# Moving an output copy, a transposed drive and the next batch's norm pieces within the state loop of a fused kernel

## What is computed

```python
def step(h, inp):
    dt_t, B_t, C_t, x_t = inp
    dA = jnp.exp(dt_t[:, :, None] * A)
    h = dA * h + (dt_t * x_t)[:, :, None] * B_t[:, None, :]
    y = jnp.einsum('bds,bs->bd', h, C_t)
    return (h, y)
...
y = y + xc * D_param
y = y * silu(z)
return jnp.einsum('bld,od->blo', y, out_proj_w)
```

## Time and profile before

| | |
|---|---|
| median of 3 runs | 1814.51 us (1811.84 to 1815.16) |
| the profiled execution | 1811.03 us, its span 1809.2 us |
| TensorE matmul, busy | 1623.4 us (90%) |
| TensorE weight load | 1052.8 us (58%) |
| VectorE | 1138.1 us (63%) |
| ScalarE | 1033.0 us (57%) |
| GpSimd | 1051.4 us (58%) |

### The profile page before, as it was taken

How to read it: one execution, slowest core, us unless ns; L and a number is a source line. 1 busy time by engine, 2 the same in 40 slices (tenths; PEclk the granted TensorE clock), 3 DMA queues, 4 the chain that set the end, 5 groups by cost and what they waited for, 6 DMA issues and landing times. The chain is left out here.

```text
span 1809.2 us, 23458 instructions
## 1 busy us (share of the span) xinstructions
PE 1623.4 (90%) x6777; PEld 1052.8 (58%) x6822; DVE 1138.1 (63%) x1344; ACT 1033.0 (57%) x2054; POOL 1051.4 (58%) x562
## 2 busy tenths in 40 slices
PE   5589998979999888999897999878999999999997
PEld 2244445644445553444563444556688888888896
DVE  2799988489898579898758999846422222222222
ACT  5868875878974888986687887431122222222222
POOL 0599890278995158999037899400355555555543
PEclk9799999999999999999998999987799999999999
DMA  3355650156652056664015575552022222222222
GB/s 105 113 184 211 222 184 1 52 190 210 233 188 94 0 162 208 208 211 175 2 65 203 197 241 192 214 222 73 25 37 39 36 40 35 35 38 38 38 31 26
DMA packets 76670, 216.14 MB, mean 119 GB/s; under 512 B 12397, under 2 KB 31158, under 8 KB 73239
## 3 DMA queue, kind: packets, MB, share of 16 engines
q1 hardware_dynamic: 60662, 196.25, 31.4%
q0 software_dynamic: 15904, 18.66, 6.5%
HBM read 193.47 MB, written 19.82 MB: 118 GB/s over the span
## 5 line engine op out<-in xcount | busy, mean ns | idle before, releaser
L477 PE MATMUL psum<-HC_sb,ident_sb 128*128 128x512 f32 x768 | 365.9, 604 | 16.4 <-DVE HC_sb L1618 8.9
L2033 ACT ACTIVATE hgt_sb<-psum_moe,b_sb 128x256 f32<-128x256 f32 (+1 forms) x312 | 116.5, 456 | 424.4 <-PE psum_moe L1933 424.4
L477 PE MATMUL psum<-experts_sb 64*128 64x512 f32 (+6 forms) x838 | 277.4, 566 | 60.7 <-DVE HC_sb L1618 20.7
L1198 ACT ACTIVATE experts_sb<-experts_sb 128x128 f32<-128x128 f32 x800 | 255.8, 388 | 36.0 <-PE psum L480 34.3
L1933 PE MATMUL psum_moe<-XGT_sb,w1s_sb 128*128 128x256 f32 (+1 forms) x1248 | 254.3, 362 | 1.3 <-DVE XGT_sb L2170 0.9
L2185 DVE TENSOR_TENSOR YS_sb<-psum_moe,b_sb 128x256 f32<-128x256 f32 x71 | 30.2, 425 | 357.3 <-PE psum_moe L1933 357.3
L1933 PE MATMUL psum_moe<-experts_sb,hgt_sb 128*128 x1136 | 251.7, 379 | 0.7 <-DVE YS_sb L2185 0.7
L1608 DVE TENSOR_TENSOR_SCAN experts_sb<-experts_sb,psum 128x1024 f32<-128x1024 f32 x100 | 227.1, 2271 | 39.7 <-PE psum L480 26.0
L1908 POOL DMA_INDIRECT out<-YS_sb,scat_sb x71 | 128.6, 1811 | 202.3 <-DVE YS_sb L2189 187.6
L1933 PEld LDWEIGHTS psum_moe<-XGT_sb,w1s_sb 128*128 128x128 f32 x1248 | 218.9, 191 | 27.1 <-DVE w1s_sb L2176 1.2
L477 PEld LDWEIGHTS psum<-HC_sb,ident_sb 128*128 128x128 f32 x768 | 141.6, 192 | 158.8 <-issue 108.6
(11 more groups left out here) (307 smaller groups left out, 2398.1 us busy)
## 6 DMA issues: line engine op xcount, KB each, us to landing
X_XT_sb<-bc_rows SPq DMA_DIRECT2D x116, 512.0 KB, 4.0
DA_sb<-bc_rows SPq DMA_DIRECT2D x80, 512.0 KB, 4.8
experts_sb<-bc_rows SPq DMA_DIRECT2D x40, 512.0 KB, 5.6
SQ_sb<-bc_rows SPq DMA_DIRECT2D x36, 512.0 KB, 5.1
T_sb<-bc_rows SPq DMA_DIRECT2D x20, 512.0 KB, 5.7
experts_sb<-w1T SPq DMA_DIRECT2D x8, 1024.0 KB, 19.4
experts_sb<-w2T SPq DMA_DIRECT2D x8, 1024.0 KB, 21.4
X_sb<-x_tok SPq DMA_DIRECT2D x5, 1024.0 KB, 6.7
```

The costliest lines, as they stand in the source:

```text
L477: return nc.tensor.matmul(o, lhsT, rhs, start=start, stop=stop, **k)
L1198: m = nc.scalar.activation(scaled_tile(c)[:, n, :], DTX_TOK[:, n, :], ACT.Copy, scale=B_TOK[:, n, c, j % NS:j % NS + 1])
L2033: m = nc.scalar.activation(HGT[:, k, 4 * h + q, 0:w], psum[:, 2 * h + q // 2, (q % 2) * 2 * P:(q % 2) * 2 * P + w], ACT.Gelu, bias=b1[:, b ...
```

## The change

Three things move; no instruction is added or taken away.

- ScalarE's `chunk_out` moves from state s = 3, behind its blocks, to s = 4, between the decay and the blocks.
- TensorE's sums at the start of chunks 1 to 3: s = 2 holds `direct` and one sum; s = 3 holds none; s = 4 holds the turned drive of s = 6, and behind it the three sums of s = 1, 2 and 3. Before, three sums stood ahead of that turned drive and one behind it.
- The norm pieces follow a list, `NORM_STATES`, which comes out as 18, 24, 26, 30 (two sums each), 32, 34, 40, 42 (two squares each, the mean at 32), 46, 48, 50, 56 (two norms each). `first_std` follows at 43, `first_small` at 44, `first_shift` at 45.

```diff
+def norm_states():
+    states = []
+    for i in range(FIRST_AT, NI):
+        blocks = sum(scaled_behind(j).get(i, 0) for j in range(NI) if is_turned(j))
+        slack = not on_pool(i - 3)
+        k = len(states)
+        room = 0 if i >= NS and i % NS in (3, 4) else 2 if slack else 1 if not blocks else 0
+        if k == 2 * NB and room and i < states[-1] + 3:
+            room = 0
+        states += [i] * min(room, NB - k % NB)
+    assert len(states) >= 3 * NB
+    return states[:3 * NB]
...
                     c_row(i)
-                    if i % NS == 1 and c:
+
+                    if not c or i % NS in (0, *range(5, NS)):
+                        sum_states(i - 1)
+                    elif i % NS == 1:
                         out_proj(c - 1)
-                        continue
-                    if i % NS == 2 and c:
+                    elif i % NS == 2:
                         direct(c)
                         sum_states(i - 2)
-                    sum_states(i - 1)
+                    elif i % NS == 4:
+                        for k in (3, 2, 1):
+                            sum_states(i - k)
...
                     decay(i)
                     if i - 2 == TOK_AT[0]:
                         dtx_tokens(0)
+                    if i >= NS and i % NS == 4:
+                        chunk_out(i // NS - 1)
                     scale_blocks(i)
-                    if i >= NS and i % NS == 3:
-                        chunk_out(i // NS - 1)
...
-                    n = (i - FIRST_AT) % NB
-                    k = (i - FIRST_AT) // NB
-                    if k == 0:
-                        first_sum(b + 1, n)
-                    if k == 1:
-                        if n == 0:
-                            first_mean(b + 1)
-                        first_square(b + 1, n)
-                    if k == 2 and n == 0:
+                    for k, at in enumerate(NORM_STATES):
+                        if at != i:
+                            continue
+                        if k < NB:
+                            first_sum(b + 1, k)
+                        elif k < 2 * NB:
+                            if k == NB:
+                                first_mean(b + 1)
+                            first_square(b + 1, k - NB)
+                        else:
+                            first_norm(b + 1, k - 2 * NB)
+                    if i == NORM_STATES[2 * NB - 1] + 1:
                         first_std(b + 1)
-                    if k == 3:
-                        first_norm(b + 1, n)
...
-                    if i == FIRST_AT + 2 * NB + NB // 2 + 1:
+                    if i == NORM_STATES[2 * NB - 1] + 3:
                         first_shift(b + 1)
...
-                    if i == FIRST_AT + 2 * NB + NB // 2:
+                    if i == NORM_STATES[2 * NB - 1] + 2:
                         first_small(b + 1)
```

More of the change, by code:

```diff
@@ L1732 @@
 TOK_AT = (2, NS - 4, 2 * NS - 4, 3 * NS - 4)
+NORM_STATES = norm_states()
 RESIDUAL_AT = (41, 43, 46, 49)
```

## The result

The changed kernel takes 1822.55 us (median of 20 runs, 1811.49 to 1825.5), the kernel before 1812.53 us beside it (median of 20). The ratio is 1.0047, with a 95% interval of 1.0036 to 1.0059: slower by about 8.5 us (the means are 8.5 us apart, the medians 10.0). The forecast was 1821.7.

The account below looks back on a forecast made before the run. VectorE, busiest engine, bounds the kernel (176.6 of 192 us). Per batch +2.45 (first_shift), -0.6 (squares and sums), -0.05 (chunk 3) give +1.8, over four batches +7.2: 1814.5 + 7.2 = 1821.7 us; range 1818.5 to 1829, with the hidden Sqrt 1811 to 1829.

Parts of the forecast that it names:

- The chunk start: Starts of chunks 1 to 3: waits move from scans to the read at s = 5; gain 0.05 us each.
- the gain stays: Rival at chunk starts: TensorE's run ends sooner, so the scans' 39 us are saved; 1782 us, chance 0.13.
- The Sqrt at 43: ScalarE at state 43: Sqrt with two table loads makes scan 44 2.2 us late per batch, bounds 1.5 to 2.6.
- the Sqrt stays hidden: Rival at state 43: ScalarE reaches the Sqrt 2.2 us sooner, scan 44 does not wait; 1812 us, chance 0.22.
- The page named in the prediction: Table loads at state 43: 1283 ns plus about 1380 ns drain per switch; scan 44 another 2.7 us late per batch.
- First_shift and the gate of chunk 2: GpSimd behind drive 45: first_shift waits for first_small and keeps the loss; gate of chunk 2 2.45 us late per batch.
- The clock at 44: TensorE idle about 2.6 us ahead of T46, clock falls: 0 to 1.6 us more per batch; a sixth of forecast's 0.65.
- The end of chunk 1: States 27 to 32: fewer squares ahead of T33, so the gate of chunk 1 comes 0.6 us earlier per batch.
- the wait at scan 28: End of chunk 1: this 0.45 us wait goes, but scan 29 starts when drive 29 ends; 0.1 us gained at most.
- The sum: Whole kernel: +2.45 - 0.6 - 0.05 = +1.8 us per batch, +7.2 us over four batches.
- The level of 1821.7: Forecast median of the changed kernel: 1814.5 for the kernel before plus 7.2 us.

Follow-up runs that it names:

- the third experiment: Changed kernel with the in-scan Sqrt of first_std made as Ln and Exp, so no table loads at state 43; 0.9959 of the kernel before.
- e2_norms_alone: Kernel before with only the new list of norm pieces, sums and chunk_out in their old order; 1.0034 of the kernel before.
- e4_c_row_first: Changed kernel with the C row of s = 5 ahead of the three sums at s = 4; 1.0045 of the kernel before.
- e5_short_out_proj: Changed kernel with the skip product of out_proj left out at chunks 0 to 2; 1.0004 of the kernel before.

## Why the prediction was right

**The chunk start.** Right in each step. T38 starts 8.72 us after out_proj (forecast 486.55 - 477.83 = 8.72), the C row stays, scans 36 and 38 don't wait, and the reads take the wait over, 12 times. The order change alone measures nothing. The rival that the gain stays would have needed slack in TensorE's rows, and there is none.

**The Sqrt at 43.** Right in place and mechanism. The blocks of state 40 start 19.25 us behind the gate of chunk 1, in both kernels (before: 495.80 and 476.55):

```profile
498.45 1.28 ACT L1218 ACTIVATE experts_sb<-experts_sb 128x128 f32<-128x128 f32 x4 [3.65 <-PE psum L496]
```

This is what the rival "the Sqrt stays hidden" would have needed earlier. Scan 44's wait of 2.5 us was forecast as 2.2. The sum up to the first load came to 9.86 and takes 10.14 (498.45 to 508.59): the load starts at the end of the blocks, without the overlap of some 0.1 us that blocks and a decay have, and the blocks of state 42 wait 0.14 us longer for T42 than was put into the sum. Loads and Sqrt take 2.91, as in the row before. The page named in the prediction (the Trainium skill, "ScalarE: Activation LUTs", What ACT_TABLE_LOAD costs) would have a drain in each switch; the trace shows none here either, and by its price (about 1380 ns for each drain) scan 44 would have waited some 5 us, an estimate.

**First_shift and the gate of chunk 2.** Right. From the gate of chunk 1 to that of chunk 2 it is 2.7 us more in three batches and 3.3 in the second; forecast 2.45. In three batches the difference is the 0.3 of scan 44. Without the stall, in the third experiment, first_shift makes this stretch 0.1 us longer (49.1 instead of 49.0), as was forecast.

**The clock at 44.** The prediction gave this case part of its chance, with 0 to 1.6 us per batch. It came in one batch of four here. TensorE's T46 with T47, in the second batch and in the third:

```profile
516.08 3.63 PE L496 MATMUL psum<-ident_sb,experts_sb 128*128 128x128 f32 x16 [2.49 <-ACT experts_sb L1218]
...
811.09 1.97 PE L496 MATMUL psum<-ident_sb,experts_sb 128*128 128x128 f32 x16 [2.49 <-ACT experts_sb L1218]
```

and a window of 2 us on each of them (us, then PE, PEld, DVE, ACT and POOL busy, the granted clock, DMA):

```profile
516.00:518.00 2.00, 1.92 (x9) 1.93 (x10) 2.00 (x3) 1.06 (x2) 1.61 (x2) 0.53 0.01 2
...
811.00:813.00 2.00, 1.91 (x17) 1.91 (x18) 2.00 (x3) 1.08 (x2) 1.59 (x2) 1.00 0.00 0
```

At 0.53, near the lower level of 1.2 GHz, the transposes take 1.7 us longer, read 45 waits 1.28 us for its C row, and 0.6 of that reaches the gate. T46 waits 2.49 to 2.52 us in every batch of the four profiled kernels that have the Sqrt at 43; a fall of the clock followed within 1.3 us of its start, or had begun up to 0.5 us ahead of it, in one batch of the changed kernel, none of e2_norms_alone, two of e4_c_row_first and three of e5_short_out_proj: 6 of 16.

**The end of chunk 1.** The sign was right, the size not: from the gate of chunk 0, the gate of chunk 1 comes 0.9 to 1.0 us earlier per batch, forecast 0.6. T33 still waits for ScalarE, 0.54 instead of 1.23:

```profile
474.17 1.09 PE L496 MATMUL psum<-ident_sb,experts_sb 128*128 128x128 f32 x8 [0.54 <-ACT experts_sb L1218]
```

In the second batch, from scan 29 to the gate, the step ahead of read 31 is 0.52 shorter, which is the forecast's part. The other 0.5 are steps shorter by 0.21 (ahead of read 29), 0.15 (ahead of scan 32) and 0.09 (ahead of the gate), and 0.05 elsewhere: waits too short to have a bracket in the rows, which the forecast did not count. That the wait at scan 28 would be taken back by drive 29 was right: scan 29 now waits 0.56 for it:

```profile
466.01 2.29 DVE L1629 TENSOR_TENSOR_SCAN experts_sb<-psum,DBX_sb 128x1024 f32<-128x1024 f32 x1 [0.56 <-POOL DBX_sb L1308]
```

**The sum.** Forecast 7.2 us in the scans, profiled 7.7, timed 8.5 with an interval of about 6.5 to 10.7. That the sum comes so close is in part luck, since two errors cancel: the loss at 44 is 2.7 to 3.3 per batch instead of 2.45, the gain at chunk 1's end 0.9 to 1.0 instead of 0.6. The level of 1821.7 is luck in part as well: it stands on a median of 1814.5 for the kernel before, which is 1812.5 over 20 runs, while the changed kernel's median lies 10.0 above that and not 7.2.

What stays open: what decides in which stretches the clock is at its lower level, and whether the 4 us of the third experiment that lie outside the scans come from that alone. The stretch ahead of the first scan also varies, from 81.2 to 83.6 us, and the clock does not explain it: the mean granted clock there is 0.90 in the kernel before (81.5 us) and 0.90 in the changed kernel (83.5).

## What to carry to other kernels

When an item is moved ahead in an engine's program and the same items still stand ahead of the next thing that is waited for, look for the reader of that next thing: here 39 us of waits went from scans to reads, and nothing was gained. A fixed piece of 2.9 us is free or dear by its place alone: it belongs where its engine idles at least that long, counting what already stands in that idle time (here four squares), and moving it should be summed against the next deadline of that engine, as a chain from the last point that stays. Such a chain was good to 0.3 us here; short waits without a bracket in the rows were worth 0.5 us a batch and are seen only by comparing the steps between starts.

## What the runs showed of the hardware

The same idle time of TensorE, 2.49 us ahead of T46, was followed by a granted clock of 0.53 in one batch and of 1.00 in another, in one execution, with the same work on either side; over four kernels a fall came at 6 of 16 such waits of 2.49 to 2.52 us. The same 378 matmuls took 80.9 us of TensorE's time in a stretch granted 0.88 and 86.7 in one granted 0.84. A logarithm between Exps needed no table load (0.44 us for logarithm and Exp), where a Sqrt needed two (2.91 us in all). In the rows of state 43 a table load starts only at the end of the instruction ahead of it (508.59 behind blocks that end at 508.58), while decay 44 (511.50 and 1.15) and the blocks behind it (512.56) overlap by 0.09 us.
